# Handing over from one expert mixture to the next: stricter waits for the first two gates, and a planner that knows of them

## The reference, cut to what matters

```python
x  = L0_attn_encoding                                   # 4 x 1024 x 128
xn = layernorm(x)
# block 0: causal attention with scores (xn R) xn^T, and 16 experts (top 2) plus a shared one
x  = x + softmax((xn @ R) @ xn.T + causal) @ xn \
       + sum_e route0[e] * ((silu(xn @ w_gate[e]) * (xn @ w_up[e])) @ w_down[e]) + shared(xn)
xn = layernorm(x)
# block 1, part one: attention with 16 heads of 8
x1 = tlin(attend(tlin(xn, q), tlin(xn, k), tlin(xn, v)), o)
# block 1, part two: rmsnorm, causal attention with 16 heads of 4 and rotary, then 8 experts (top 2)
res = xn + causal_attend(rmsnorm(xn) @ ...) @ w_up
t   = rmsnorm(res)
y   = sum_e route1[e] * ((silu(t @ w1[e]) * (t @ w3[e])) @ w2[e])
x  = x + x1 + res + y
```

## Time and profile before

| | us |
|---|---|
| median of 3 executions | 2166.03 |
| lowest, highest | 2165.41, 2168.79 |
| the profiled execution (one of the three) | 2165.41 |
| its span, from first to last instruction | 2163.5 |
| around the span | 1.9 |

### The profile page before, as it was taken

One profiled execution on the slowest core, in us unless ns is written; L12 is line 12 of the kernel. 1 busy time (PEld: TensorE's weight loads), 2 busy tenths in 40 slices (PEclk: granted clock), 3 DMA queues, 4 the chain that ended last, 5 costly groups with the idle time before them and its releaser, 6 DMA issues. The chain is left out here.

```text
span 2163.5 us, 33722 instructions
## 1 busy us (share of the span) xinstructions
PE 2036.6 (94%) x11936; PEld 945.2 (44%) x11936; DVE 1549.2 (72%) x2807; ACT 1215.0 (56%) x2325; POOL 131.7 (6%) x251
## 2 busy tenths in 40 slices
PE   6869999999999999998999999999999999999889
PEld 4622333435655233344665423343565632334356
DVE  5678887746788887673778878775577978867155
ACT  2224777773522677776352467777544166777721
POOL 2000011100000000110000000110000000111000
PEclk9957999999999999999999999999999999999989
DMA  5160101002171100000136010010106301010011
GB/s 192 35 175 1 30 17 35 23 2 65 58 188 34 30 16 26 17 17 27 54 116 138 11 31 16 26 31 2 55 25 181 78 7 30 18 29 17 2 48 41
DMA packets 66631, 105.16 MB, mean 49 GB/s; under 512 B 11136, under 2 KB 20288, under 8 KB 66080
## 3 DMA queue, kind: packets, MB, share of 16 engines
q1 hardware_dynamic: 66464, 103.03, 17.8%
HBM read 79.26 MB, written 22.94 MB: 47 GB/s over the span
## 5 line engine op out<-in xcount | busy, mean ns | idle before, releaser
L1339 ACT ACTIVATE prob<-ps 128x512 f32<-128x512 f32 (+3 forms) x1792 | 867.3, 555 | 355.3 <-PE ps L1605 265.9
L1145 DVE TENSOR_REDUCE row_max<-ps 128x1 f32<-128x1024 f32 x512 | 606.5, 1219 | 106.2 <-PE ps L1574 105.4
L1605 PE MATMUL ps<-q_stack,k_stack 96*128 96x512 bf16 (+4 forms) x1792 | 552.9, 363 | 25.0 <-ACT prob L1339 17.0
L1574 PE MATMUL ps<-k_stack,q_stack 96*128 96x512 bf16 (+4 forms) x1792 | 534.4, 372 | 27.9 <-DMA q_stack<-scratch_q 15.6
L1142 DVE CUSTOM_DVE_ANT_0 tmp<-ps,const_b 128x128 f32<-128x128 f32 (+7 forms) x512 | 371.5, 756 | 131.3 <-PE ps L1574 117.8
L1630 PE MATMUL ps<-prob,v_ones 128*32 128x512 f32 (+3 forms) x3584 | 437.9, 561 | 2.5 <-ACT prob L1339 2.5
L1605 PEld LDWEIGHTS ps<-q_stack,k_stack 96*128 96x128 bf16 (+1 forms) x1792 | 172.4, 98 | 361.3 <-ACT prob L1339 232.1
L1574 PEld LDWEIGHTS ps<-k_stack,q_stack 96*128 96x128 bf16 (+1 forms) x1792 | 152.7, 99 | 375.2 <-DVE row_max L1142 94.9
L1490 PEld LDWEIGHTS ps<-wd,prob 128*128 128x128 f32 (+1 forms) x1600 | 206.6, 193 | 77.6 <-issue 65.1
L1286 ACT ACTIVATE prob<-ps 128x512 f32<-128x512 f32 x128 | 76.4, 597 | 270.1 <-PE ps L1515 269.7
L1490 PE MATMUL ps<-wd,prob 128*128 128x128 f32 (+1 forms) x1600 | 212.6, 277 | 2.1 <-DVE prob L1041 2.1
(11 more groups left out here) (169 smaller groups left out, 1501.7 us busy)
## 6 DMA issues: line engine op xcount, KB each, us to landing
spread_w<-scratch_r SPq DMA_DIRECT2D x128, 128.0 KB, 3.0
spread_w<-scratch_r SPq DMA_DIRECT2D x64, 256.0 KB, 3.5
k_stack<-scratch_k SPq DMA_DIRECT2D x48, 256.0 KB, 6.8
q_stack<-scratch_q SPq DMA_DIRECT2D x48, 256.0 KB, 7.6
scratch_k<-tmp SPq DMA_DIRECT2D x36, 256.0 KB, 2.8
k_stack<-scratch_k SPq DMA_DIRECT2D x96, 64.0 KB, 2.2
q_stack<-scratch_q SPq DMA_DIRECT2D x96, 64.0 KB, 2.2
scratch_k<-tmp SPq DMA_DIRECT2D x36, 128.0 KB, 2.9
```

Source lines behind the costliest of these rows:

```text
L1145: dve.tensor_reduce(nm[G % 2][:, t, j:j + 1], ring_pair(r)[:], AX_X, ALU.max).then_inc(s["ring_used"], 1)
L1339: act.activation(p_slot(v, j)[:, lo - at:hi - at], bank(UNIT_BANKS[u % 3])[:, 0:hi - lo], ACT.Exp, scale=SCALES[kind_of(G)]).then_inc(s["p ...
L1574: ins = pe.matmul(ring_pair(r)[:, lo:hi], queries(G, j)[:, t * P:(t + 1) * P], keys(G, j)[:, lo:hi], start=True, stop=True)
L1605: ins = pe.matmul(dst[:, 0:hi - lo], keys(G, j)[:, kc * P:(kc + 1) * P], queries(G, j)[:, lo:hi], start=True, stop=True)
```

## The change

In the planner, the tuple handed over consists of the last activation (or first product), the last product, the last scaled product and the last `mixed`, and gate 0 of the next mixture comes after all four; up 0 comes after the last `mixed`; `spread` 0 and `down` 0 lose their own entries. In every mixture gate n = 1 comes after step 0's activation (mixture 1) or product (mixture 0). In the built kernel gates n = 0 and n = 1 of every mixture wait for `gu_ready` k instead of k - 1: gate 0 for all products of the mixture before, gate 1 for the product of step 0 of its own mixture.

```diff
-    def mixture(w, b, which, xT, routed, halves, loads, freed=()):
+    def mixture(w, b, which, xT, routed, halves, loads, freed=(), mixed=None):
...
-                at = do("PE", "gate", 0.88, last(taken, 2), last(scaled, 2), last(ups), xT if n == 0 else None, freed[n] if freed and n < 2 else None)
+                at = do("PE", "gate", 0.88, last(taken, 2), last(taken) if n == 1 else None, last(scaled, 2), last(ups), xT if n == 0 else None, *(freed if n == 0 else ()))
                 gates.append(do("ACT", "gate", 0.6, at, last(scaled, 2), last(gates)))
-                ups.append(do("PE", "up", 0.0 if which == 0 and n % C0 == C0 - 1 else 0.88, at, last(scaled), freed[1] if freed and n == 0 else None))
+                ups.append(do("PE", "up", 0.0 if which == 0 and n % C0 == C0 - 1 else 0.88, at, last(scaled), mixed if n == 0 else None))
...
-                hids.append(do("DVE", "spread", 0.7 if at else 0.05, scaled[-1], last(downs), last(hids), freed[2] if freed and n == 0 else None, *at))
+                hids.append(do("DVE", "spread", 0.7 if at else 0.05, scaled[-1], last(downs), last(hids), *at))
...
-                downs.append(w.op("PE", ("down", b, which, n - 1), 1.05, hids[n - 1], last(out), last(downs), freed[3] if freed and n == 1 else None))
+                downs.append(w.op("PE", ("down", b, which, n - 1), 1.05, hids[n - 1], last(out), last(downs)))
...
-        return out, (scaled[-2], scaled[-1], downs[-1], out[-1]), loads
+        return out, (taken[-1], scaled[-1], hids[-1], out[-1]), loads
...
-            mixture(w, b - 1, 1, xT, routed, (joined, joined), loads, freed)
+            mixture(w, b - 1, 1, xT, routed, (joined, joined), loads, freed, mixed[-1])
...
                 elif n >= 2:
                     pe.wait_ge(s["sg_ready"], k - 1)
-                elif k >= 2:
-                    pe.wait_ge(s["gu_ready"], k - 1)
+                elif k:
+                    pe.wait_ge(s["gu_ready"], k)
```

## The result

The changed kernel took 2180.67 us as the median of 6 executions (2176.29 to 2183.12); the kernel before, run beside it, took 2166.29 (2165.22 to 2168.79). The ratio is 1.0064 with a 95% interval of 1.0051 to 1.0078: slower by 14 us. The profiled execution took 2177.56 us, 3.1 under that median.

The account below looks back on a forecast made before the run. TensorE's own instructions were taken to set the pace. Hand-overs 6.9, last weave 2.8 and weave 0 0.8 sum to 10.5 us on 2165.4, so 2175.9, stated as 2176; 8 in 10 from 2167 to 2183, forecast chance 0.55.

Parts of the forecast that it names:

- my 1.0 to 4.0: Each hand-over in weaves 1 to 3: delay range, +1.0 without the low clock, +4.0 with all of it at low clock.
- My 2.3 us each: Three hand-overs: gate 1 waits for product 0 with `turn_r` queued behind, so `turn` ends +2.3 us later; 6.9 in all.
- I let the low clock end where it ended before: Hand-over: half-rate clock after gate 1's wait assumed over at about 582.5, so gate 1 and `turn_r` end at 583.0.
- without the low clock +1.0: Hand-over at full clock: gate 1 and `turn_r` end at 581.8, copy until 583.0, `turn` until 584.1; +1.0 us.
- the order does not change: Last weave: gate 1 planned only 0.2 later with nothing else ready, so the engines' order stays.
- my 2.8: Last weave: gate 1 waits for product 0, delaying `turn_r` by 1.5 us, plus 1.3 of low clock; +2.8 (1.5 to 3.2).
- +0.8: Weave 0: gate 1 waits for product 0, leaving an idle place for a full one; +0.8 us (0.9 at most).
- Mixture (b, 0) in weaves 1 to 3: Gate 1 there: `turn_c`, now placed first, covers the wait, cost 0; bare, up to 1 us each.
- Given back: Rival: idle of 3.66 us ahead of `q_stack` takes each hand-over's 2.3; 2169.0, or 2167.7 without last-weave low clock; chance 0.13.
- Faster through a sooner product: Rival: `turn_c` ahead of gate 1 brings routes and product 0 3.4 us sooner at hand-overs; 2161.9; chance 0.10.
- The spreading clock: Rival: at the four new idles all work up to `turn` runs at low clock, 1.7 us more each; 2182.7; chance 0.12.
- A costlier order: Rival: reshuffle holds up a block-0 attention tile by 1.0 to 2.5 us in each of three weaves; 2179 to 2183.5; chance 0.10.

Follow-up runs that it names:

- kernel 2: The changed kernel's planner with the old built waits of the kernel before; 2169.38 us, ratio 1.0006.
- kernel 4: The changed kernel with the planner told the built wait, so gate 1 comes after product 0 in mixture 1 too; 2171.13 us, ratio 1.0010.
- kernel 8: The changed kernel with five unread matmuls ahead of gate 1's wait at three hand-overs, and gate 1's activation planned after the routes' copy; 2176.95 us, ratio 1.0049.
- kernel 9: The changed kernel with five unread matmuls ahead of gate 1's wait at the three hand-overs only; 2179.18 us, ratio 1.0057.
- kernel 11: The kernel before with two unread matmuls ahead of `turn_r`'s wait at the three hand-overs; 2164.20 us, ratio 0.9985.
- kernel 1: The kernel before with only the built waits changed, planner and order kept; 2184.10 us, ratio 1.0072.
- kernels 7: The changed kernel with the layernorm's first part planned behind product 0 of mixture 1; 2172.68 us, ratio 1.0027.
- kernel 5: The changed kernel with the new built waits in mixture 1 only, mixture 0 keeping the old ones; 2179.22 us, ratio 1.0067.
- Kernels 10: The changed kernel with the last weave's planner clause and built waits put back as before; 2175.31 us, ratio 1.0044.
- kernels 6: The kernel before with the layernorm's first part planned behind product 0 of mixture 1; 2164.65 us, ratio 0.9993.
- 12: The kernel before with the layernorm's first part planned behind product 0 of mixture 1, and two unread matmuls ahead of `turn_r`'s wait at hand-overs; 2162.90 us, ratio 0.9984.

## Why the prediction was right, and where its steps were not

**The direction, the place and the order were right.** The order at the hand-over came out as written, with gate 1 idle for 4.4 us behind L1029 three times. Product 0 came when I said: gate 1 started 9.51 us after `turn_h`, against 580.02 - 570.57 = 9.45 in the working. Kernels 2 and 4 show that the wait costs at the hand-over, and only with `turn_r` queued behind it.

**The hand-over was mis-sized, inside my 1.0 to 4.0.** My 2.3 us each was to the end of `turn`; measured so it is 3.5, 2.4 and 2.4. To its start the same working gives 584.4 - 581.89 = 2.5, and measured is 3.4, 3.2 and 3.1 (9.7 over three). Two steps of it failed. "I let the low clock end where it ended before" is the first: in weave 1 it lasted into `turn`, so `turn_r` ended 584.48 - 571.42 = 13.06 us after `turn_h` in place of 583.0 - 570.57 = 12.43, +0.6. In weaves 2 and 3 it ended at 12.49 and 12.75, nearly as I had it. The second: I counted `turn_r` and its copy and did not look at what stands ahead of the copy in ScalarE's list. Behind gate 1 that is 0.60 + 1.28 + 0.21 us, and the copy began 0.56 us after `turn_r` ended, where I had 0.2. At the full clock the same queue costs 1.1 (kernel 8 against 9), so my "without the low clock +1.0" measured 14.7 - 12.5 = +2.2 to the end of `turn`. I put the clock at 1.3 of the 2.3; it is 0.4 to 1.0, and it was being paid before too: 0.5 to 0.9 in the kernel before (kernel 11). The difference between kernels 9 and 11, both at the full clock, is 3.4 us, as large as that between the two kernels. Of it 2.6 is `turn_r`, which starts 10.46 us after `turn_h` in place of 7.84, and the rest lies between `turn_r` and `turn`. The loss is the queue, on two engines.

**The last weave: "the order does not change" was wrong.** The planner moved product 0 ahead on VectorE, and on TensorE an up and a gate ahead of `turn_r` and another pair ahead of `turn_h`. In the order that I assumed the wait costs 3.3 (kernel 1), for my 2.8: gate 1 stood idle for 2.89 us, and it and `turn_r` ran at the low clock. In the real one it is 2.9 by the order, since the routes are late and `project` now waits for the copy of `turn_h`, and in this profile 1.5 more by the clock behind the first down (2.05 us against 1.13); in the profiles of kernels 7, 8 and 9 the low clock behind gate 1's wait costs 1.9 to 2.2 on top of that. That my 2.8 lies next to the 2.9 is an accident.

**Weave 0: +0.8 stays open.** Weave 1 starts 0.9 us later (`encode` at 496.11, before 495.20), but 0.7 of that is there already at gate 0 of mixture (0, 0) (23.78 against 23.06), ahead of every changed wait. So the edit's own part is about 0.2 there (472.33 us against 472.14 from that gate to `encode`), but over all kernels this stretch takes 471.06 to 474.16, so neither this nor kernel 5 can resolve it.

**Mixture (b, 0) in weaves 1 to 3: 0, as forecast.** In weave 1 `turn_c` (from 500.02 on) covers the wait, and gate 1 has no idle:

```profile
501.91 1.12 PE L1515 MATMUL ps<-xT,wg 128*128 128x512 f32 x2
```

`turn_c` to `turn_h` grew by 0.86 in each weave, and `encode` to `turn_c` shrank by 0.91 (3.91 against 4.82): the swapped gate, counted once on either side. Bare, I had the wait at up to 1 us each; kernel 1 measured 1.3.

**The sum.** By the profiles: 9.7 + 4.4 + 0.9, and the attention behind weave 2 gave back 3.4 (from `turn` to the next `encode` 433.11 against 436.53), behind weave 3 it took 0.8; with 0.2 less in what leads to the hand-overs that is 12.2, the difference of the spans. TensorE, VectorE and ScalarE run the same instructions in the same order there, so the 3.4 is not another order; most of it is the clock. Before, two stretches there ran at a low clock that after ran at 1.00; the kernel before, then the changed one, at the same distances from `turn`:

```profile
1102.35:1106.35 4.00, 4.00 (x14) 2.80 (x13) 1.82 (x2) 2.62 (x4) 0.00 (x0) 0.70 0.51 136
1118.35:1122.35 4.00, 4.00 (x17) 2.74 (x16) 3.04 (x3) 0.79 (x2) 0.00 (x0) 0.57 0.41 149
```

```profile
1109.75:1113.75 4.00, 4.00 (x16) 2.33 (x17) 1.82 (x2) 2.96 (x4) 0.00 (x0) 1.00 0.32 61
1125.75:1129.75 4.00, 4.00 (x23) 2.80 (x22) 3.87 (x6) 3.08 (x4) 0.00 (x0) 1.00 0.29 110
```

The first of them is the end of the hand-over's own low clock, over `turn` and the gate behind it, so that part (1.2 us) belongs to the hand-over. Why the second came in one profile and not in the other is open. Kernels 10 and 11 have 432.56 and 433.26 there, the changed kernel's order and the old one, so the order doesn't decide it. My sum was 10.5, where the profiles differ by 12.2 and the medians by 14.4: the direction and the range held, and the sum was 3.9 us under the difference of the medians.

**The rivals.** Given back: no; from `turn` to the next `encode` weave 1 takes 434.11 us against 434.16. The idle ahead of the first piece is 0.6 shorter there (3.04 against 3.66), and the rest of the stretch took that up again. Faster through a sooner product: no; product 0 kept its place on VectorE. The spreading clock: in part, it held for the whole stretch in weave 1, but kernel 9 shows that it isn't most of what costs. A costlier order: not in the block-0 attention; it was the last weave whose order changed.

## What to carry to other kernels

Price a new wait at the head of an in-order list by what stands behind it on its own engine, and then do the same on the next engine down: here gate 1's activation, a table load and a square root stood ahead of the copy that the path needed. When a planner's dependence (on the activation) is earlier than the built wait (on the product), it will place an item where it blocks; telling it the true one took the three hand-overs back to their old length. Watch the covered waits too: mixture 0's cost nothing only because the new order put `turn_c` ahead of them. Run the planner for every stretch before saying that an order stays, since a constraint of 0.2 us moved two engines' lists in the last weave.

## What the runs showed of the hardware that was not expected

A gap of 2.38 us in TensorE's work is followed by the low clock at all three hand-overs of the kernel before, and filling it with unread matmuls keeps the clock at 1.00 and gains 0.5 to 0.9 us of a hand-over (kernel 11). The Trainium skill (TensorE: Matmul & The Clock Gate, HAM oscillation) has it as a rule to leave no gaps above a few microseconds. By it there should have been nothing to gain from this gap; the runs disagree. Nor does the length of the gap decide by itself. In kernel 2 a gap of 1.84 us was followed by an up of 1.12 us in weave 1, at the full clock, and by one of 2.07 in weave 3, at the low one. In kernel 4 a gap of 2.69 was followed by a gate of 2.05 in weave 1 and by one of 1.10 in weave 3:

```profile
1623.97 1.10 PE L1515 MATMUL ps<-tT,wg 128*128 128x512 f32 x2 [0.67 <-DVE prob L1029]
```

Where the gap ahead of `turn_r` was at most 1.09 us (kernels 6, 7, 11 and 12), the clock stayed at 1.00 at all twelve hand-overs. Code that is the same can differ by more than an effect under study: from the last `turn_c` to gate 0 of the last weave, where all kernels have the same code, the profiles show 16.15 us (before) to 19.01 (kernel 4), by where the low clock falls. Whole stretches of a single profile should not be compared more closely than that.
